# Rounded three-product projections for queries and keys in the first attention, and three score tiles at a time in its last chunk

## What is computed

```python
x = x + _L0_attn_ref(_layernorm(x, axis=-1), ...)
x = x + _L0_ffn_ref(_layernorm(x, axis=-1), ...)

def _L0_attn_ref(x, W_qkv, b_qkv, W_out, b_out):      # 16 heads of 64
    qkv = (x @ W_qkv + b_qkv).reshape(b, s, 3, H, D)
    k = k + pos_enc[None, :, None, :]
    attn = jax.nn.softmax(jnp.einsum('bqhd,bkhd->bhqk', q, k) / scale, axis=-1)
    return jnp.einsum('bhqk,bkhd->bqhd', attn, v).reshape(b, s, H * D) @ W_out + b_out

def _L0_ffn_ref(src, ...):                            # 16 heads of 8, then 4 experts of 512
    attn = ...                                        # a second attention, over the same tokens
    x = _layer_norm(src + attn @ Wo + bo, ln1_g, ln1_b)
    expert_idx = jnp.remainder(jnp.floor(keys).astype(jnp.int32), N_EXPERTS)
    ...                                               # the chosen expert's two layers
    return _layer_norm(x + ff_out, ln2_g, ln2_b)
```

## Time and profile before

| | us |
|---|---|
| median of 3 runs | 2144.91 (2139.06 to 2145.79) |
| the profiled execution | 2144.52 |
| its span, first to last instruction | 2142.7 |

### The profile page before, as it was taken

The page is one execution under the profiler, slowest core; times in us unless marked ns, Lnnn a source line. Parts: engine busy times, 40 slices in busy tenths (PEclk is TensorE's granted clock), DMA queues, the critical chain, the costliest instruction groups (busy, mean ns, idle before and its releaser), DMA issues.

```text
span 2142.7 us, 35861 instructions
## 1 busy us (share of the span) xinstructions
PE 2060.6 (96%) x12074; PEld 945.5 (44%) x12074; DVE 1692.1 (79%) x2739; ACT 1702.3 (79%) x2299; POOL 1284.4 (60%) x777
## 2 busy tenths in 40 slices
PE   6999999999999999999999989999999999999996
PEld 2544445445444445454454433333333433443445
DVE  7677787877877878777887837789999999999903
ACT  1678888888888888888888984388878878888883
POOL 1588898897997987988988795333032024016003
PEclk7899999999999999999999998599999999999998
DMA  3000000000000000000000100000000000000000
GB/s 105 20 16 20 27 16 31 16 17 30 16 28 19 16 31 16 27 20 16 31 16 27 40 16 20 1 1 2 2 1 1 2 2 7 1 2 6 1 2 11
DMA packets 32039, 36.33 MB, mean 17 GB/s; under 512 B 12340, under 2 KB 23228, under 8 KB 31736
## 3 DMA queue, kind: packets, MB, share of 16 engines
q1 hardware_dynamic: 31864, 34.03, 5.1%
HBM read 32.46 MB, written 1.43 MB: 16 GB/s over the span
## 4 chain that ended last, share of the span: by engine, by line
PE 80%; ACT 7%; DVE 6%; issue 3%; POOL 3%; DMA 0%; DVEq 0%; ACTq 0%; POOLq 0%
PE acc_o L538 18%; PE scores L516 14%; PE acc_o L658 11%; PE scores L644 10%; PE ring L491 8%; ACT prob L846 3%; DVE mxp L1521 3%; PE ring L624 2%; POOL accp L1016 2%; PE ring L708 2%; PE ring L717 2%; ACT prob L868 2%; PE ring L468 2%; ACT scores L853 2%; PE ring L456 2%
## 5 line engine op out<-in xcount | busy, mean ns | idle before, releaser
L1404 DVE TENSOR_REDUCE mxp<-ring 128x1 f32<-128x512 f32 x1024 | 656.3, 685 | 231.3 <-PE ring L491 214.6
L1016 POOL TENSOR_TENSOR accp<-accp,prob 128x1024 f32<-128x1024 f32 x318 | 799.8, 2515 | 54.5 <-ACT prob L846 11.0
L868 ACT ACTIVATE prob<-scores 128x512 f32<-128x512 f32 x1024 | 545.3, 601 | 135.6 <-PE scores L644 132.9
L846 ACT ACTIVATE prob<-scores 128x1024 f32<-128x1024 f32 x512 | 520.0, 1016 | 147.1 <-PE scores L516 127.9
L516 PE MATMUL scores<-q_all,k_all 64*128 64x512 f32 x3072 | 545.4, 409 | 7.2 <-ACT scores L853 4.9
L1521 DVE TENSOR_REDUCE mxp<-ring 128x1 f32<-128x512 f32 x789 | 510.7, 684 | 52.4 <-PE ring L624 39.9
L853 ACT ACTIVATE scores<-minus_all 128x1024 f32<-128x1024 f32 x510 | 525.2, 1030 | 24.2 <-ACT prob L846 0.8
L538 PE MATMUL acc_o<-prob,v 128*64 128x512 f32 x2048 | 500.3, 609 | 2.9 <-ACT v L828 2.9
L491 PE MATMUL ring<-k_all,q_all 64*128 64x512 f32 x1024 | 392.8, 432 | 10.1 <-DVE mxp L1404 5.5
L516 PEld LDWEIGHTS scores<-q_all,k_all 64*128 64x128 f32 x3072 | 336.2, 186 | 84.8 <-ACT scores L853 41.2
L644 PE MATMUL scores<-q_all,k_all 32*128 32x512 f32 x1024 | 308.1, 494 | 12.7 <-ACT prob L868 8.5
(11 more groups left out here) (197 smaller groups left out, 1553.9 us busy)
## 6 DMA issues: line engine op xcount, KB each, us to landing
minus_all<-m_dram SPq DMA_DIRECT2D x32, 512.0 KB, 3.6
rec<-rec_dram SPq DMA_DIRECT2D x60, 128.0 KB, 2.8
w_all<-w_pairs SPq DMA_DIRECT2D x1, 1344.0 KB, 11.2
x<-x SPq DMA_DIRECT2D x4, 256.0 KB, 3.8
pos_sb<-pos SPq DMA_DIRECT2D x1, 1024.0 KB, 7.6
w_all<-w SPq DMA_DIRECT2D x1, 1024.0 KB, 5.6
minus_all<-w SPq DMA_DIRECT2D x4, 256.0 KB, 3.6
q_all<-m_rows SPq DMA_DIRECT2D x64, 2.0 KB
```

Source lines behind the costliest of these rows:

```text
L846: nc.scalar.activation(prob[:, T % SLOTS1, :, :], sc[T % 2][:, :, :], ACT.Exp, scale=SCALE1).then_inc(exp_done, 1)
L868: nc.scalar.activation(prob2[:, h // 2, T % 2, h % 2, :], sc2[place % 3], ACT.Exp, scale=SCALE2).then_inc(exp2_done, 1)
L1016: nc.gpsimd.tensor_tensor(accp[:, k % 2], accp[:, k % 2], prob[:, T % SLOTS1], ALU.add).then_inc(pool_acc, 1)
L1404: done(nc.vector.reduce_max(mxp1[k % 2][:, h * QT + q, kc:kc + 1], bank[:], AX.X), ("max", k, q, kc, h))
```

## The change

**Projections.** From the second pair on, a projection of queries or keys is three rounded products accumulated in one bank (high weights by high tokens, high by low, low by high) in place of one full product. POOL makes the parts: of the tokens once, ahead of its first add (`split_tokens`, eight operations of 128x512), and of a pair's weights in two operations of 128x128 behind its second add of a chunk: the queries' weights in the second chunk of the pair before, the keys' in the third chunk of the pair before that. The parts of the tokens use the memory that later holds the parts of the experts' weights.

**Last chunk.** In chunk 31 a step has six `max2` tiles in two runs of three, and none ahead of its first scores. The 16 additional ones are the first 16 of `EARLY_TILES`, which stood among the first scores of the second attention. Q2 of block 1 moves from step 3 of chunk 31 to step 7 of chunk 30.

**Second attention.** The tiles are taken with the block of keys in the outer loop instead of the block of queries. V2 of blocks 2 and 3 move from steps 3 and 6 of block 0 to steps 0 and 1, the four K2 of block 0 from steps 5, 7, 8, 9 to 2, 3, 5, 7. One expert item moves from block 15 to the last step of block 14, and block 15's nine are spaced wider.

```diff
--- before.py
+++ after.py
@@ -89,9 +89,9 @@
 
 LATE1 = {(2, 0): [("rows2",)],
          (CHUNKS1 - 2, 2): [("T2", 0)], (CHUNKS1 - 2, 3): [("K2", 0, 0)], (CHUNKS1 - 2, 4): [("Q2", 0)],
-         (CHUNKS1 - 2, 6): [("K2", 1, 0)],
+         (CHUNKS1 - 2, 6): [("K2", 1, 0)], (CHUNKS1 - 2, 7): [("Q2", 1)],
          (CHUNKS1 - 1, 0): [("V2", 0)], (CHUNKS1 - 1, 1): [("T2", 1)], (CHUNKS1 - 1, 2): [("K2", 0, 1)],
-         (CHUNKS1 - 1, 3): [("Q2", 1)], (CHUNKS1 - 1, 5): [("K2", 1, 1)], (CHUNKS1 - 1, 6): [("T2", 2)],
+         (CHUNKS1 - 1, 5): [("K2", 1, 1)], (CHUNKS1 - 1, 6): [("T2", 2)],
          (CHUNKS1 - 1, 7): [("K2", 0, 2)]}
 
 
@@ -102,9 +102,10 @@
 
     if k < LAST1:
         return []
-    tiles = [("max2", 0, h, q, kc) for kc in range(2) for q in range(QT) for h in (2, 3, 0, 1)]
+    first, second = ([("max2", 0, h, q, kc) for q in range(QT) for h in (2, 3, 0, 1)] for kc in range(2))
+    tiles = first + EARLY_TILES[:16] + second
     n = 2 * j + half
-    return tiles[2 * n:2 * n + 2]
+    return tiles[3 * n:3 * n + 3]
 
 
 def seeded1(T):
@@ -130,6 +131,8 @@
         if cp:
             tiles += [("max", *cp, h) for h in range(2)]
         tiles += tiles_late1(k, j, half)
+    if k == LAST1:
+        return [], tiles[:3], tiles[3:]
     return tiles[:1], tiles[1:3], tiles[3:]
 
 
@@ -175,15 +178,16 @@
 
 
 MAX2_STEPS = 11
+EARLY2 = STEPS2 - MAX2_STEPS
+EARLY_TILES = [("max2", 1, h, i % QT, i // QT) for i in range(EARLY2) for h in (2, 3, 0, 1)]
 KEYS2 = (0, 2, 1, 3)
 SPLIT_BY_DVE = [("K2", 0, 3)]
-EARLY2 = STEPS2 - MAX2_STEPS
 
 
 def tiles2(n, t):
 
     to = n + 1 if t < MAX2_STEPS else n + 2
-    q, kc = divmod((t + EARLY2) % STEPS2, NC)
+    kc, q = divmod((t + EARLY2) % STEPS2, QT)
     if to >= BLOCKS2:
         return [], []
     return [(to, h, q, kc) for h in (2, 3)], [(to, h, q, kc) for h in (0, 1)]
@@ -201,6 +205,12 @@
 
 
 FF_STEPS = (2, 4, 5, 6, 7, 8, 9, 10, 12, 13, 14)
+FF_ENDS = {BLOCKS2 - 2: (2, 4, 5, 6, 7, 8, 9, 10, 12, 13, 14, 15), BLOCKS2 - 1: (0, 2, 3, 5, 6, 8, 10, 12, 14)}
+
+
+def ff_steps(n):
+
+    return FF_ENDS.get(n, FF_STEPS)
 
 
 def items2(n, t):
@@ -208,10 +218,11 @@
     c, g = divmod(n, GROUPS)
     items = []
     if n < 2:
-        if n == 0 and t in (3, 6):
-            items.append(("V2", {3: 2, 6: 3}[t]))
-        if t in (5, 7, 8, 9):
-            items.append(("K2", n + 2, (5, 7, 8, 9).index(t)))
+        if n == 0 and t < 2:
+            items.append(("V2", 2 + t))
+        steps = (2, 3, 5, 7) if n == 0 else (5, 7, 8, 9)
+        if t in steps:
+            items.append(("K2", n + 2, steps.index(t)))
     if t == 1 and n > 0:
         items.append(("o", n - 1))
     if t == (3 if n > 0 else 4) and n + 2 < BLOCKS2:
@@ -221,8 +232,8 @@
     if c > 0:
         if g == 0:
             items += {5: [("ot", c - 1)], 7: [("wo", c - 1)], 14: [("xt", c - 1)], 15: [("rk", c - 1)]}.get(t, [])
-        elif t in FF_STEPS:
-            k = FF_STEPS.index(t) + len(FF_STEPS) * (g - 1)
+        elif t in ff_steps(n):
+            k = ff_steps(n).index(t) + sum(len(ff_steps(b)) for b in range(GROUPS * c + 1, n))
             items += experts(c - 1)[k:k + 1]
     return items
 
@@ -231,10 +242,7 @@
     def tiles(kc):
         return [("max2", 0, h, q, kc) for q in range(QT) for h in (2, 3, 0, 1)]
     return ([("sums", LAST1), ("V2", 1), ("y", LAST1)] + tiles(2) + [("T2", 3), ("K2", 0, 3), ("K2", 1, 2)] + tiles(3)
-            + [("fin2", 0), ("K2", 1, 3)] + EARLY_TILES[:4])
-
-
-EARLY_TILES = [("max2", 1, h, *divmod(i, NC)) for i in range(EARLY2) for h in (2, 3, 0, 1)]
+            + [("fin2", 0), ("K2", 1, 3)] + EARLY_TILES[16:])
 
 
 def end2():
...
@@ -309,7 +317,11 @@
         v2 = v1[:].rearrange("p a t n -> p (a t n)").rearrange("p (t h n) -> p t h n", t=NT, h=H2)
         w1_sb = w_all[:].rearrange("p a n -> p (a n)")[:, 0:E * FF].rearrange("p (e n) -> p e n", e=E)
 
-        w1hi, w1lo = sb("w1hi", [128, E, FF], F32R), sb("w1lo", [128, E, FF], F32R)
+        parts_hi, parts_lo = sb("parts_hi", [128, S], F32R), sb("parts_lo", [128, S], F32R)
+        w1hi, w1lo = (part[:].rearrange("p (e n) -> p e n", e=E) for part in (parts_hi, parts_lo))
+
+        xhi, xlo = parts_hi, parts_lo
+        wq_parts, wk_parts = sb("wq_parts", [128, 2, 128], F32R), sb("wk_parts", [128, 2, 128], F32R)
         x2hi, x2lo = q_all[:, NC:NC + 2, :], q_all[:, NC + 2:NC + 4, :]
         o2 = accp[:].rearrange("p a b c -> p (a b c)").rearrange("p (t n) -> p t n", t=NT)
         rounded = sb("rounded", [128, CW], F32R)
...
@@ -450,14 +464,30 @@
                     last = nc.tensor.transpose(bank[:, q * 128:(q + 1) * 128], xn_tok[:, c * QT + q, :], ident[:])
                 end(last, ("T", c))
 
+            def rounded_proj(bank, w, b):
+
+                pe.wait_ge(xlo_ready, b + 1)
+                cols = slice(b * CW, (b + 1) * CW)
+                for n, (part, tokens) in enumerate(((0, xhi), (0, xlo), (1, xhi))):
+                    last = nc.tensor.matmul(bank[:], w[:, part, :], tokens[:, cols], start=(n == 0), stop=(n == 2))
+                return last
+
             def q_proj(k):
                 p, c = k // NC, k % NC
                 bank = begin(("Q", k))
+                if p > 0:
+                    pe.wait_ge(wq_lo, p)
+                    end(rounded_proj(bank, wq_parts, c), ("Q", k))
+                    return
                 end(nc.tensor.matmul(bank[:], w_all[:, p, 0:128], xnt[:, c * CW:(c + 1) * CW], start=True, stop=True),
                     ("Q", k))
 
             def k_proj(p, b):
                 bank = begin(("K", p, b))
+                if p > 0:
+                    pe.wait_ge(wk_lo, p)
+                    end(rounded_proj(bank, wk_parts, b), ("K", p, b))
+                    return
                 end(nc.tensor.matmul(bank[:], w_all[:, p, 128:256], xnt[:, b * CW:(b + 1) * CW], start=True, stop=True),
                     ("K", p, b))
 
@@ -786,12 +816,8 @@
                 item2(it)
             pe.wait_ge(o_copied, CHUNKS1)
             ahead = [(0, 2), (0, 3), (0, 0), (0, 1), (1, 2), (1, 3)]
-            for x in ahead[:2]:
+            for x in ahead:
                 scores2(*x)
-            for k, x in enumerate(ahead[2:]):
-                scores2(*x)
-                for it in EARLY_TILES[4 * k + 4:4 * k + 8]:
-                    item2(it)
             for n in range(BLOCKS2):
                 for t in range(STEPS2):
                     T = STEPS2 * n + t
@@ -1177,8 +1203,34 @@
             for h in range(2):
                 nc.gpsimd.memset(onesw[64 * h:64 * h + 1, :].bitcast(F32), 1.0).then_inc(blank, 1)
                 pool.wait_ge(blank, 3 + h)
+            def split_weights(p, first, to, hi, lo, last_use):
+
+                pool.wait_ge(pairs_dma, 16 * 4)
+                if p > 1:
+                    wait_full(pool, last_use)
+                w = w_all[:, p, first:first + 128]
+                nc.gpsimd.tensor_tensor(to[:, 0, :], w, zero[:].to_broadcast([128, 128]), ALU.subtract).then_inc(hi, 1)
+                pool.wait_ge(hi, p)
+                nc.gpsimd.tensor_tensor(to[:, 1, :], w, to[:, 0, :].bitcast(F32), ALU.subtract).then_inc(lo, 1)
+
+            def split_query_weights(p):
+                split_weights(p, 0, wq_parts, wq_hi, wq_lo, ("Q", NC * p - 1))
+
+            def split_key_weights(p):
+                split_weights(p, 128, wk_parts, wk_hi, wk_lo, ("K", p - 1, NC - 1))
+
+            def split_tokens(b):
+                wait_free(pool, ("T", b))
+                cols = slice(b * CW, (b + 1) * CW)
+                nc.gpsimd.tensor_tensor(xhi[:, cols], xnt[:, cols], zero[:].to_broadcast([128, CW]), ALU.subtract).then_inc(xhi_ready, 1)
+                pool.wait_ge(xhi_ready, b + 1)
+                nc.gpsimd.tensor_tensor(xlo[:, cols], xnt[:, cols], xhi[:, cols].bitcast(F32), ALU.subtract).then_inc(xlo_ready, 1)
+
             for b in range(NC):
                 split_keys(0, b)
+            split_key_weights(1)
+            for b in range(NC):
+                split_tokens(b)
             def late(k, j):
                 for it in LATE1[k, j]:
                     split_of(it)
@@ -1193,6 +1245,10 @@
                         deviations(0, k - CHUNKS1 + 2, stats2, rstd_ready)
                     if t == (POOL_ADDS if k < LAST1 else 6) and k > 0:
                         normalise(k - 1)
+                    if t == 2 and k % NC == 1 and k // NC + 1 < PAIRS:
+                        split_query_weights(k // NC + 1)
+                    if t == 2 and k % NC == 2 and k // NC + 2 < PAIRS:
+                        split_key_weights(k // NC + 2)
                     if t == 3 and last_item1(k, 0) and last_item1(k, 0)[0] == "K":
                         split_keys(*last_item1(k, 0)[1:])
                     if t == 8 and k == CHUNKS1 - 2:
@@ -1201,8 +1257,6 @@
                         late(k, 4)
                     if t == 5 and k == LAST1:
                         late(k, 2)
-                    if t == 7 and k == LAST1:
```

(4 more changed lines are left out.)

4 lines of the change are left out of this document (3 added, 1 removed).

## The result

The changed kernel takes 2149.91 us (median of 8 runs, 2147.54 to 2151.73), the kernel before 2145.44 (8 runs): ratio 1.0025, 95% interval 1.0014 to 1.0037. It is slower by 4.5 us where the forecast was 4 us faster: inside the range, on the other side of no change. Of the kernel before a few executions end near 2140 and most at 2145 to 2147, so a difference of two medians and the ratio, which goes by all runs, may differ by a microsecond or more (by the ratio the change costs 5.4 us).

The account below looks back on a forecast made before the run. PE was taken to bound the first attention, with POOL 0.5 us from being waited for, and DVE's reductions the turn. −9.0 + 6.1 + 8.0 − 7.0 − 2.2 + 0.5 = −3.6 us gave 2141 us, range 2129 to 2152.

Parts of the forecast that it names:

- The projections' saving: First attention: three rounded products take 0.89 us instead of 1.05, 0.16 less for each of 56 projections, −9.0 us.
- POOL's work in the second chunk of a pair: Rounding query weights takes POOL 1.0 us where it has 0.5 of room; DVE and PE wait, +6.1 us (0 to 10).
- POOL's additional microsecond is free: Rival: POOL's 0.5 us of room and the bank's cover hold, +6.1 goes to 0, 2135 us; chance 0.17.
- Last chunk, turn and clock: Threes in chunk 31 +8.0 us, turn without tiles −7.0 (net +1.0), clock up sooner through early V2 −2.2.
- The rest: Block 0's K2 queueing behind ACT's buffer and the late expert item in the last block: +0.5 us together (−1 to +2).
- The clock is back before the second attention's steps: Rival: clock rises ahead of block 0; transposes, K2 and slow steps run full speed, 6 us more, 2135 us; chance 0.16.
- The clock falls in the last chunk: Rival: PE's stops in chunk 31 lower the clock, six more stretches cost 11 us, 2152 us; chance 0.15.
- The three products save nothing: Rival: loading 128x128 weights three times loses the 9.0 us while POOL's part stays, 2150 us; chance 0.04.

Follow-up runs that it names:

- experiments 1: The kernel before with the projections' part of the change alone: 2147.52 us against 2145.40, ratio 1.0016.
- 2: Projections' part alone, query weights rounded in a pair's last chunk, a chunk and more earlier, into a second buffer; against the kernel before 2139.52 us to 2145.40, ratio 0.9972.
- Experiment 3: Projections' part alone, POOL rounding the query weights behind its fourth add instead of its second; 2146.39 us against 2146.50 for the kernel before, ratio 1.0014.
- 4: As Experiment 3, with POOL's first add of chunks 6, 10, ... waiting for DVE's second add; 2143.24 us against 2145.64 for the kernel before, ratio 0.9998.
- experiments 13 to 15: Kernel before with Q2's move plus: threes and early V2/K2 (2144.56 us); threes and rounded products, weights moved (2141.20); those products and early V2/K2, no threes (2130.03).
- experiment 14: Kernel before with rounded products (weights rounded in a pair's last chunk), Q2's move and tiles in threes, V2 and K2 as before: 2141.20 us, ratio 0.9978.

## Why the prediction was wrong

**The projections' saving** was right: 0.89 us, 0.14 to 0.18 less in each step that has one. But not all of the 56 gain. In the traces without POOL's stall a pair is 0.9 to 1.1 us shorter, not 8 × 0.16 = 1.3: the keys' projection in step 0 of a pair's first two chunks gains 0.16 to 0.18 there, and step 1 loses 0.14 to 0.18. ACT copies `oraw` at the start of step 0, and its exponentials and maxima then come one behind the other; that it is ACT which paces step 1 was only argued.

**The step that failed is POOL's work in the second chunk of a pair** (+6.1 forecast, about +10.6 measured: 8.3 + 2.3 between experiments 1 and 2). Where it was placed, whom it delays, and that PE stops behind DVE's reductions was right, and so was the size of this first stall: 1.0 us in step 7, where I had 0.9. What I had not followed is what comes behind it. The sum stopped at the first wait. DVE's second add, 5 us later, had a lead of 0.1 us over POOL's next one, and each delay of DVE in these runs flipped the order, 0.65 us as well as 1.00. I had written that the add "beside POOL's next work, is some 0.2 us longer", of the first (its rows say 0.36, and 0.37 came); for the second it is 1.4. This lost race costs 0.66 us in each of the six chunks, 4.0 of the 4.5 us that the term was too small. Experiments 3 and 4 show it: in 3 the lost race is 0.95 of the 1.4 us a chunk, and with DVE first by force, in 4, these are gone.

The first stall was right by luck. I took the price of the pair from multiplications at a time when DVE did something else; in its place it stood beside DVE's add and took 1.9 us, past the upper bound of 1.5. But POOL's way from its first add to the end of its last became only 1.0 us longer (577.65 to 611.04 against 576.21 to 608.64), since the pair met an add of DVE that one of POOL's own adds had met before: the two adds beside it took 4.74 us where they had taken 5.71. Experiment 3, where the pair takes 0.9, shows that the wrong price did not matter.

*POOL's additional microsecond is free* was wrong for the same reason: the room in front of the second add was 0.1 us, not 0.5 + 0.45.

**Last chunk, turn and clock** look right in the table: +9.8 - 7.1 - 3.9 = -1.2, and the forecast was +8.0 - 7.0 - 2.2 = -1.2. The experiments show two errors that cancel, so this agreement is luck. The early V2 alone is worth 5 to 6 us, not 2.2: the lower level ended within 4 us of the first values, in step 0. (The 1.74 us that I took for a V2 at half speed is one in which the clock rose; wholly at the lower level it is 2.08.) The threes cost 2.7 us alone and 5.3 beside the early V2, not 1.0. Beside the early V2 the shorter turn brings the first values sooner but not the clock, which comes a step later. I added terms which share one cause, the moment at which the clock comes back.

**The rest** (+0.5) missed the queue behind the late expert item: block 15 was right (+0.4), but I followed the item only to the exponentials beside it, not through its statistics to ACT's queue. It costs another 1.0 to 1.9 us.

**The other rivals.** *The clock is back before the second attention's steps*: no, first values are at the lower level (1.91 us) in every trace. *The clock falls in the last chunk*: it did, for about a third of the price that I gave it. Over chunk 31 it is 0.90 in the changed kernel and 0.96 in the one before (rows in experiments 13 to 15). By the prediction's own sum that is 0.10 × 2 × 54.0 = 11 us at the lower level against 4, so some 3.6 us more of lost time (an estimate), where the rival had 11; my +8.0 had no such term, and the last two chunks came out at +9.8. The rule that the Trainium skill has for this ("TensorE: Matmul & The Clock Gate", section "A second HAM failure mode: psum-queue depth-cycling") agrees with the trace in direction: PE cycles through the banks in threes with waits for DVE, and the clock falls more often. It did not make the kernel the 2152 of the rival.

*The three products save nothing*: no.

**Does it add up?** The projections' part alone +2.1 by the medians, all the rest +0.8, together +2.9; measured +4.5. Some 1.6 us are left over so; they are as large as the intervals, and by the ratios, which go by all runs, nothing is left: 1.0016 and 1.0008 make 1.0024, measured 1.0025.

## What to carry to other kernels

A small piece of work on an engine with a microsecond of room is not priced by its own length. Follow the delay through at least the next two things that its waiter does, and look there for pairs of instructions that start within a few tenths of a microsecond of each other on DVE and POOL: the order of such a pair is a step in the cost. Put such work in a stage where the engine has several microseconds of slack, even if it needs a second buffer. And when several edits act on the stretch in which the clock is low, they are one term and not several. In this kernel the longest full-array products were worth most at the start of the dense stretch that follows.

## What was not expected of the hardware

- Two adds of 128x1024 on DVE and POOL that overlap: the first to start takes its own time (1.22 us on DVE, 2.37 on POOL). DVE's, when it is second, ends 1.1 us after POOL's (2.61 and 2.91 us long); POOL's, when it is second, takes 1.0 us longer (3.36).
- A 128x128 operation of POOL took 0.39 us alone and 1.39 beside DVE's add (L1208 and L1212).
- With V2's eight full products in step 0 of block 0 the clock was up about 4 us after the first values (1370.03 to 1374); the same eight among DVE-paced tiles at the turn left it low (2.08 us for the eight, the lower level). In experiment 14 it was up after 11 us with no V2 before it.
- The same order of work in chunk 31 took 44.5, 46.1 and 47.0 us with the granted clock at 1.00, 0.96 and 0.93.
